# Products of the identity in four of TensorE's waits: behind the first transposes and around the end of the experts

## The reference

```python
x = _layernorm(x + _L0_attn_ref(x, ...))          # linear attention over 16 heads of 64, then a GELU block 256-1024-256
x = _layernorm(x + _L0_xattn_ref(x, ctx, ...))    # softmax attention to 375 context rows per batch
x = _layernorm(x + _L0_ffn_ref(x, ...))           # 8 experts, 2 per token, 17 slots per expert and batch
```

```python
y_tok = y.reshape(E * B * cap, C)[flat_idx.reshape(-1)].reshape(B, T, K, C)
y_tok = y_tok * (p_flat * keep.astype(x.dtype))[:, :, None]
return y_tok.reshape(B, T, K, C).sum(axis=2)
```

## Time and profile before

| | |
|---|---|
| median of 3 executions | 2250.69 us |
| fastest and slowest of them | 2245.33 us, 2253.78 us |
| the profiled execution | 2256.79 us |
| its span (first to last instruction) | 2255.1 us |
| mean granted TensorE clock in it | 0.981 |
| TensorE busy | 2176.0 us, 96% |
| VectorE, ScalarE, GpSimd busy | 67%, 60%, 34% |

### The profile page before, as it was taken

How to read it: one execution, slowest core, us unless ns; L and a number is a source line. 1 busy time by engine, 2 the same in 40 slices (tenths; PEclk the granted TensorE clock), 3 DMA queues, 4 the chain that set the end, 5 groups by cost and what they waited for, 6 DMA issues and landing times. The chain is left out here.

```text
span 2255.1 us, 57833 instructions
## 1 busy us (share of the span) xinstructions
PE 2176.0 (96%) x20778; PEld 1665.9 (74%) x20778; DVE 1505.9 (67%) x4396; ACT 1361.9 (60%) x3178; POOL 760.9 (34%) x1335
## 2 busy tenths in 40 slices
PE   7999999999998999999999999999999999989997
PEld 4776876867867677777777777777777777878876
DVE  4555545455447687777778787777777777376547
ACT  6546456356355576767767676767676767455434
POOL 1211221222215244544545454545454544100003
PEclk9999999999999999999999999999999999699988
DMA  5000000000001100000000000000000000052202
GB/s 162 20 1 1 0 0 0 0 0 0 15 19 39 42 10 16 11 16 11 16 10 16 10 17 10 16 10 17 10 16 10 16 3 2 1 141 85 75 1 66
DMA packets 45732, 51.44 MB, mean 23 GB/s; under 512 B 19120, under 2 KB 37664, under 8 KB 45504
## 3 DMA queue, kind: packets, MB, share of 16 engines
q1 hardware_dynamic: 45504, 48.45, 7.3%
HBM read 44.78 MB, written 3.67 MB: 21 GB/s over the span
## 5 line engine op out<-in xcount | busy, mean ns | idle before, releaser
L1744 POOL TENSOR_SCALAR arena<-arena,p_rec 112x375 f32<-112x375 f32 x512 | 303.0, 593 | 572.6 <-DVE p_rec L1607 569.2
L1611 DVE TENSOR_TENSOR pt_lo<-b_t,pt_hi 125x336 f16<-125x336 f32 x512 | 258.5, 505 | 234.7 <-ACT pt_hi L1502 234.5
L64 PE MATMUL b_pb<-arena 128*125 128x512 f16 (+1 forms) x1364 | 385.1, 303 | 14.1 <-ACT arena L1454 5.7
L65 PE MATMUL b_pb<-arena 128*125 128x512 f16 (+1 forms) x1364 | 377.7, 298 | 0.0
L66 PE MATMUL b_pb<-arena 128*125 128x512 f16 (+1 forms) x1364 | 377.4, 297 | 0.0
L1496 ACT ACTIVATE arena<-arena,neg_max 112x375 f32<-112x375 f32 x512 | 312.3, 610 | 1.6 <-DVE neg_max L1593 1.6
L1593 DVE CUSTOM_DVE_ANT_0 arena<-b_s,arena 112x375 f32<-112x375 f32 x512 | 273.5, 534 | 11.6 <-PE b_s L1353 6.8
L1362 PEld LDWEIGHTS b_t<-ident,arena 112*125 112x125 f32 x1536 | 237.3, 190 | 37.5 <-issue 1.4
L1362 PE MATMUL b_t<-ident,arena 112*125 112x112 f32 x1536 | 252.1, 273 | 0.0
L1502 ACT ACTIVATE pt_hi<-b_t 125x336 f16<-125x336 f32 x512 | 228.3, 446 | 6.0 <-PE b_t L1362 5.9
L64 PEld LDWEIGHTS b_pb<-arena 128*125 128x125 f16 (+1 forms) x1364 | 147.3, 108 | 95.7 <-issue 27.1
(11 more groups left out here) (284 smaller groups left out, 5717.3 us busy)
## 6 DMA issues: line engine op xcount, KB each, us to landing
arena<-in_L_ffn_W_dram SPq DMA_DIRECT2D x16, 1024.0 KB, 7.4
arena<-in_ctx_dram SPq DMA_DIRECT2D x32, 375.0 KB
out_dram<-c_z SPq DMA_DIRECT2D x8, 448.0 KB, 3.2
x_sb<-in_x_dram SPq DMA_DIRECT2D x1, 3136.0 KB, 18.8
ff<-in_L_attn_w_dram SPq DMA_DIRECT2D x2, 1024.0 KB, 7.6
ff<-in_L_xattn_Wkv_dram SPq DMA_DIRECT2D x2, 1024.0 KB, 5.4
arena<-in_mask_BxS_bf_dram SPq DMA_DIRECT2D x32, 41.0 KB, 2.6
a_raw<-in_L_attn_wq_dram SPq DMA_DIRECT2D x1, 1024.0 KB, 5.3
```

What stands on the lines that cost most here:

```text
L64: pe.matmul(out, lh, rh, start=first, stop=False)
L65: pe.matmul(out, lh, rl, start=False, stop=False)
L1611: dve.tensor_tensor(pt_lo[:, (H * b + h) % NPT, :], t_ps[h % 2][0:JP, 0:JT * T], pt_hi[:, (H * b + h) % NPT, :], ALU.subtract).then_inc(pt ...
L1744: pool.tensor_scalar(p32[:, h % 4, :], p32[:, h % 4, :], p_rec[:, h % 4:h % 4 + 1], 0.0, ALU.mult, ALU.add).then_inc(p_norm_done, 1)
```

## The change

A new helper issues n products of the identity with itself: the float32 identity read as float16, 128x128 as weights, 128x256 as the moving operand, into a PSUM bank. It is called at four places, all in TensorE's program:

- 22 products in `layer1`, between the first transposes and the first query tile, into the bank `o_ps[0]`;
- 8 at the end of `experts`, into the bank of the last expert's first output tile, behind a wait until ScalarE has taken that tile;
- 4 at the start of `combine`, ahead of the first transposes, into `o_ps[1]`;
- 4 in `combine` behind the second batch's transposes, ahead of the first `bring_back`, into `o_ps[1]`.

```diff
+def keep_busy(pe, ps, ident, n):
+
+    busy = ident[:, :].bitcast(F16)
+    for _ in range(n):
+        pe.matmul(ps[:, 0:2 * P], busy[:, 0:P], busy, start=True, stop=True)
...
+        FILL = 22
...
             turn(0, 0)
+            keep_busy(pe, o_ps[0], ident, FILL)
             project_q(0, range(KI))
...
+        FILLED, FILL = (2 * USES - KD) % NPB, 8
...
             each(pe, body)
+            pe.wait_ge(pb_free[FILLED], freed(E // 2 - 1, 1, FT))
+            keep_busy(pe, pb[FILLED][:, 0, :], ident, FILL)
...
+        FILL = 4
...
                 for q in range(G4):
                     turn(G4 * g + q, q)
+                    if is_first(g) and q == 1:
+                        keep_busy(pe, o_ps[1], ident, FILL)
                     if not (is_first(g) and q == 0):
                         bring_back(G4 * g + q - 1, (q - 1) % G4)
 
+            keep_busy(pe, o_ps[1], ident, FILL)
             groups(pe, body)
             bring_back(B - 1, G4 - 1)
```

More of the change, by code:

```diff
@@ L1830, in layer3 @@
                                buf_hi, buf_lo, weights_high, weights_low, load_expert, sb_in, psum_in, sem)
-            experts(nc, passed, (w1_hi, w1_lo, w2_hi, w2_lo), h_hi, w_lo_done, weights_high, weights_low, load_expert, b1, b2,
+            experts(nc, ident, passed, (w1_hi, w1_lo, w2_hi, w2_lo), h_hi, w_lo_done, weights_high, weights_low, load_expert, b1, b2,
                     buf_hi, buf_lo, y_t, sb_in, psum_in, sem)
@@ L2010, in _, with experts @@
             take(NG - 1)
-def experts(nc, passed, split_weights, h_hi, w_lo_done, weights_high, weights_low, load_expert, b1, b2, buf_hi, buf_lo, y_t, sb_in, psum_in, sem):
+def experts(nc, ident, passed, split_weights, h_hi, w_lo_done, weights_high, weights_low, load_expert, b1, b2, buf_hi, buf_lo, y_t, sb_in, psum_in, sem):
     stack = ExitStack()
```

## The result

The changed kernel is slower, not faster: **2266.76 us** median of 6 executions (2257.57 to 2278.47), against 2249.43 us (2245.05 to 2253.78, 6 executions) for the kernel before. The ratio is **1.0072, 95% interval [1.0053, 1.0091]**. The forecast was 2246.8 us with a range up to 2252.6; the time lies 14 us above that range.

The account below looks back on a forecast made before the run. It took half-clock stretches, chiefly 17.0 us in the way back with TensorE busy, as the bound. Saving 8.4 less 0.5 for products, head 0, gave 7.9; half, 3.9, off the 2250.69 median gave 2246.8 us, range 2240.0 to 2252.6.

Parts of the forecast that it names:

- Both ends, 2.0 us earlier and 1.4 us later, come to nothing further on. [...] I take 0: Head of layer 1: the 22 products move the query work by -2.0 to +1.4 us, without effect on the total.
- The cover that it named: Head: the third weights' transfer, queued behind 3136 KB of x, leaves their split at 52.26 despite small shifts in issue.
- The way back: After the experts: added products keep the clock full, batches take 1.50 us instead of 2.9, at best 8.4 us saved.
- where 8 were forecast: Sign in the way back: the first store comes some 8 us earlier, counted from the experts' end.
- The 16 products were put at 0.5 us: Experts' end and way back: the 8, 4 and 4 products cost 0.1, 0.1 and 0.3 us at full clock.
- 7.9 stood in the sum: Way back of an execution like the profiled one: 8.4 us saved less 0.5 us for the products.
- half of the saving, 3.9 us: Way back: the median execution gains half of the full 7.9 us, since the half-clock stretch varies between executions.
- a bad example: Whole kernel: the profiled execution, 2256.79 us, lies 6.1 above the median, the way back's half-clock stretch possibly part of it.
- the rival of a median with hardly such a stretch: Way back: the change repairs only unlucky executions, so the median becomes 2251.2 us; chance 0.16.
- The clock falls all the same: Way back: the clock still falls, or a little later, despite the products, giving 2249 to 2251 us; chance 0.15.
- slower at the start of the way back: There the added products run at half clock and delay the last stage by 1.8 us, giving 2252.5 us; chance 0.09.
- The head counts after all: Head: if the third weights usually land before 52.26, add -2.0 to +1.4 us to the other cases; no separate chance.

Follow-up runs that it names:

- e3: Only the 22 products at the head of layer 1, added to the kernel before: 2258.56 us, ratio 1.0026 [1.0000, 1.0051].
- e5: The kernel before plus 44 semaphore increments at the very start of TensorE's program, no products: 2256.65 us, ratio 1.0018 [1.0009, 1.0027].
- e6: The kernel of e3 with 100 semaphore increments ahead of its 22 products: 2255.21 us, ratio 1.0022 [1.0010, 1.0034] to the kernel before.
- e1: The kernel before, unchanged, measured once more: 2253.04 us against 2253.95, ratio 1.0001 [0.9980, 1.0021].
- e4: Only the 8 + 4 + 4 products around the experts' end, added to the kernel before: 2251.51 us, ratio 0.9985 [0.9964, 1.0005].
- e9: Only ten products in the last group of layer 1, added to the kernel before: 2249.90 us, ratio 0.9994 [0.9975, 1.0012].
- e11: Only 64 products, four per head in layer 2's last batch, added to the kernel before: 2245.46 us, ratio 0.9970 [0.9953, 0.9987].
- e2: The changed kernel, unchanged, measured a second time against the kernel before: 2258.64 us, ratio 1.0021 [1.0001, 1.0041].
- e10: The changed kernel, unchanged, measured a third time against the kernel before: 2259.21 us, ratio 1.0042 [1.0025, 1.0059].
- e7: The kernel before plus 8 + 4 + 4 products around the experts' end and ten in layer 1's last group: 2249.78 us, ratio 0.9988 [0.9979, 0.9997].
- e8: The kernel of e7 plus 64 products, four per head in layer 2's last batch: 2246.54 us, ratio 0.9981 [0.9966, 0.9995] to the kernel before.
- e12: The kernel of e8 with two instead of four products per head in that batch: 2243.83 us, ratio 0.9971 [0.9951, 0.9991] to the kernel before.

## Why the prediction was wrong, point by point

**The step that failed: "Both ends, 2.0 us earlier and 1.4 us later, come to nothing further on. [...] I take 0".** The head was priced by what its products take and by the clock beside them. The cover that it named is real, though not as fixed as it said: the split of the third weights still waits for its transfer, which lands 1.0 us later, counted from the first transposes, because it was issued 2.1 us later (23.02 us behind them instead of 20.92). What was missing is that the 22 products are also 44 instructions, and move the place in the program at which TensorE's code is fetched. In group 7 of layer 1, 650 us later, this puts a fetch into the load of the weights: ScalarE waits 1.5 us longer, TensorE 1.4, and in all five such profiles the clock then falls for 13.6 to 17 us. The term that was put at 0 is 4.6 us in the median when the head's products stand alone (e3, interval 0 to 11.5 us). Shown: the long wait follows the count of instructions, not the products (e5, e6), and comes exactly where the 16 KB fetch starts 3.7 to 3.9 us into the load (the packets above). Argued from counts alone (5 of 5 against 2 of 9): that the longer wait brings the clock down, and with it most of the 6.3 us that group 7 lost in the profiled pair.

A direct effect of the products at the head isn't shown. From the first transposes to the end of group 0 before, e1, e4, e9 and e11 need 85.5 to 85.9 us; after, e2, e3, e10 and e6 need 86.6 to 89.5, the larger two (e2 and e10) with 3.4 and 6.8 us at half clock from 58 and 54 us on. But kernels without these products have such times too: e5 88.3 with 3.4 us at half clock at 57, e7 86.4 with the longer load of the value weights, e8 and e12 95.1 and 95.6 with 20.45 us at half clock.

**The way back, right in its mechanism.** The clock stayed at full level, the batches kept 1.50 us and the stores 6.7. The first store is issued 14.75 us after the experts' last product (2205.58 - 2190.83) instead of 22.20 (2205.32 - 2183.12), so 7.45 us earlier where 8 were forecast. The queue's rows, before's and after's:

```profile
2205.32 46.34 SPq L2318 DMA_DIRECT2D out_dram<-c_z  x8
```

```profile
2205.58 46.76 SPq L2334 DMA_DIRECT2D out_dram<-c_z  x8
```

The 16 products were put at 0.5 us and cost 0.25. In the profiled pair the stage gave 7.1 us, where 7.9 stood in the sum.

**Its share of the median was put too high.** I took half of the saving, 3.9 us. By itself (e4) it gave 2.4, with an interval from 8.1 us of gain to 1.1 of loss; 2 of 7 profiles without the products had the stretch, and 2/7 of 7.1 is 2.0 us. The profile of before was a bad example, as the prediction suspected, and the rival of a median with hardly such a stretch was nearer than its chance of 0.16 said. e1 shows it: unchanged code, and other stretches at half clock. That agrees with what the prediction quoted from the Trainium skill, "TensorE: Matmul & The Clock Gate", Part 1, that the number of slow matmuls in one kernel differs from run to run; why it does, no run here shows.

**The rivals.** "The clock falls all the same" and "slower at the start of the way back" did not happen. The slower case was looked for in the wrong place: beside the added products, where everything was small, and not behind them in the program. "The head counts after all" had the right place to begin and the wrong mechanism and size (-2.0 to +1.4; e3: +4.6 in the median).

**The chances.** 0.02 for slower by over 0.5% rested on there being no mechanism worth 9 us. One profile shows neither the spread of the clock (before's executions on one chip cover 20 us, 2244.87 to 2264.92) nor where a fetch falls after an edit. With both in view the range should have reached to about 2265.

**What stays open.** Why the first measurement shows 1.0072 and the two others 1.0021 and 1.0042. Its executions had a mean clock of 0.9787, some 97 us at half clock; by the slope that is 7 us more than before's 80 on another chip. Which stretches these were isn't in the one profile taken. And why the clock fell in the last group of e1 and e6 behind a short wait.

## What to carry to other kernels

An added instruction costs its time, and it can move the instruction fetches behind it; where a program leaves a loop into new code beside a load that an engine waits for, look there in the profile, however far from the edit. Products that nobody reads pay where the clock is low in every profile (here the last batch of layer 2: 64 for an estimated 6.7 us, 4.5 us net in the median of e11), and hardly where it is low in one execution of several. Before pricing a stretch at half clock, find out in how many executions it is there: the spread of the times of an unchanged kernel says more of that than one profile.

## What the runs showed of the hardware that was not expected

- A shift of 44 instructions on TensorE lengthened a wait for a 1024 KB load by 1.4 to 1.5 us (3.3 to 3.6 us before, 4.8 to 4.9 after), 650 us behind it; a shift of 144 did not.
- One 16 KB packet of instructions, 0.95 us long, that started 3.7 to 3.9 us into that load held the load's last seven 4 KB packets back by 1.2 to 1.5 us (5 of 5 profiles); one that started 4.6 us or more behind its issue, at its very end or after it, held back nothing (9 of 9).
- Over the later passes of a loop the queue of TensorE's instructions moved nothing for some 450 us.
- An execution's time followed its time at half clock: 0.36 to 0.44 us per us in four sets of executions of the unchanged kernel (23 to 35 each), with 74 to 80 us at half clock in the mean.
- A semaphore increment at the start of TensorE's program took about 0.15 us (21 more of them, first matmul at 10.94 instead of 7.73), more than a full-clock product of the identity (0.104 to 0.117 us: 2.57 us for the 22).
- Where TensorE's records were dense (28.29 of 30.65 us) but made of transposes and short products, the clock was at half in all profiles without added products; with four products of the identity in each head the mean of 1940 to 1975 us was 0.95 (e8) and 0.80 (e11), in before 0.55.
